# Maxima products of the first attention as four 32-query products on column tiles, for either row half

## The reference, cut to what matters

```python
scores = jnp.einsum('bhqd,bhkd->bhqk', q, k) / SCALING
att = jax.nn.softmax(scores, axis=-1)
out = jnp.einsum('bhal,bhlv->bhav', att, v)
```

## Time and profile before

| | |
|---|---|
| median of 3 runs | 1328.86 us (1328.58 to 1329.69) |
| the profiled execution | 1327.18 us, its span 1325.14 us |
| PE, share of the span busy | 91% |
| DVE | 75% |
| ACT | 63% |
| POOL | 20% |
| scores, L725, first to last start | 116.2 to 769.4 us |
| maxima, L614, first to last start | 95.2 to 743.0 us |

### The profile page before, as it was taken

How to read it: one execution, slowest core, us unless ns; L and a number is a source line. 1 busy time by engine, 2 the same in 40 slices (tenths; PEclk the granted TensorE clock), 3 DMA queues, 4 the chain that set the end, 5 groups by cost and what they waited for, 6 DMA issues and landing times. The chain is left out here.

```text
span 1325.1 us, 32172 instructions
## 1 busy us (share of the span) xinstructions
PE 1204.9 (91%) x13377; PEld 607.5 (46%) x13377; DVE 999.6 (75%) x1256; ACT 837.6 (63%) x1447; POOL 260.2 (20%) x373
## 2 busy tenths in 40 slices
PE   6977999999999999999999978888899799899980
PEld 4641333333323232233323345555799566688870
DVE  5879999999999999999999546765775788433324
ACT  3643888888888888888888845565222466533331
POOL 4200220000101001000010011100573222145560
PEclk9986999999999999999999989998998899999995
DMA  4764123232233322323311112000010211223317
GB/s 144 204 203 98 28 67 75 46 78 66 58 81 82 69 66 57 81 54 65 80 43 73 74 54 61 23 17 17 18 45 28 71 37 36 60 79 102 103 41 193
DMA packets 75229, 95.36 MB, mean 72 GB/s; under 512 B 13236, under 2 KB 44684, under 8 KB 74052
## 3 DMA queue, kind: packets, MB, share of 16 engines
q1 hardware_dynamic: 69996, 83.19, 24.4%
q0 software_dynamic: 5088, 10.12, 2.5%
HBM read 54.30 MB, written 38.56 MB: 70 GB/s over the span
## 5 line engine op out<-in xcount | busy, mean ns | idle before, releaser
L614 DVE TENSOR_REDUCE b_mx<-psum 128x2 f32<-128x1024 f32 x507 | 596.0, 1219 | 36.7 <-PE psum L558 27.9
L668 ACT ACTIVATE b_exp_ring<-psum 128x512 f32<-128x512 f32 x1024 | 540.0, 598 | 121.6 <-PE psum L725 120.8
L725 PE MATMUL psum<-b_q,b_k 75*32 75x512 bf16 x4096 | 315.4, 384 | 1.3 <-ACT b_exp_ring L668 1.1
L699 PE MATMUL psum<-b_exp_ring,b_v 128*32 128x512 f32 x2048 | 266.3, 595 | 0.7 <-ACT b_exp_ring L668 0.7
L557 PE MATMUL psum<-b_k,b_q 64*128 64x512 bf16 x512 | 188.4, 396 | 21.8 <-DVE b_mx L614 12.2
L558 PE MATMUL psum<-b_ko,b_qo 64*128 64x512 bf16 x512 | 188.4, 396 | 0.0
L725 PEld LDWEIGHTS psum<-b_q,b_k 75*32 75x32 bf16 x4096 | 86.5, 95 | 173.6 <-ACT b_exp_ring L668 112.3
L557 PEld LDWEIGHTS psum<-b_k,b_q 64*128 64x128 bf16 x512 | 47.3, 93 | 229.8 <-issue 132.7
L744 POOL CAST b_top<-b_mt 16x128 bf16<-16x128 f32 x32 | 8.9, 279 | 574.5 <-DVE b_mt L622 574.5
L1839 ACT ACTIVATE e_hT<-psum,e_b 128x358 f32<-128x358 f32 (+3 forms) x96 | 53.6, 559 | 75.4 <-PE psum L1859 72.0
L699 PEld LDWEIGHTS psum<-b_exp_ring,b_v 128*32 128x32 f32 x2048 | 60.8, 111 | 55.7 <-issue 9.6
(11 more groups left out here) (279 smaller groups left out, 1457.2 us busy)
## 6 DMA issues: line engine op xcount, KB each, us to landing
b_q<-q_ops SPq DMA_DIRECT2D x48, 192.0 KB
b_k<-k_ops SPq DMA_DIRECT2D x48, 192.0 KB
k_ops<-a_k SPq DMA_DIRECT2D x20, 256.0 KB, 3.4
x_disp<-b_zeros SPq DMA_DIRECT2D x13, 320.0 KB
e_x<-x_disp SPq DMA_DIRECT2D x8, 520.0 KB
v_ops<-a_vs SPq DMA_DIRECT2D x4, 1024.0 KB, 5.1
b_v<-v_ops SPq DMA_DIRECT2D x16, 256.0 KB
av_out<-b_acc SPq DMA_DIRECT2D x128, 32.0 KB, 1.7
```

The costliest lines, as they stand in the source:

```text
L614: nc.vector.reduce_max(mx[:, d % 2, :, i // 2, i % 2], pair, AX.X).then_inc(sem("b_max_done"), 1)
L668: act.activation(ex[:, n % E_RING, :], g.bank(5 + n % 3), ACT.Exp, scale=ATT_SCALE)\
L699: last = nc.tensor.matmul(AV[32 * i:32 * i + 32, :], v[s][:, at_v:at_v + 32], ex[:, (4 * group + i) % E_RING, :], start=(kb == 0), stop=(k ...
L725: last = nc.tensor.matmul(g.bank(5 + n % 3)[keys, :], k[s][0:XROWS, h, kb * P + 32 * j:kb * P + 32 * j + 32], q[s][0:XROWS, h, half * BANK ...
```

## The change

Both products of an item are cut by queries: each becomes four products of 32 queries, whose results lie on 32 partitions each of the same bank. The first four take the even head (row half 0), the next four the odd head (row half 64). The last one is returned, so the semaphore still counts one for an item. The streamed operand of 512 keys is the same for the four.

```diff
 def maxima_scores(g, q, k, qo, ko, n, p, i):
 
-    t, keys = slice(i // 2 * P, i // 2 * P + P), slice(i % 2 * BANK, i % 2 * BANK + BANK)
-    g.nc.tensor.matmul(g.bank(2 * (n % 2)), q[0:MROWS, 2 * p, t], k[0:MROWS, 2 * p, keys], start=True, stop=True)
-    return g.nc.tensor.matmul(g.bank(2 * (n % 2) + 1), qo[MROWS:P, p, t], ko[MROWS:P, p, keys], start=True, stop=True)
+    keys = slice(i % 2 * BANK, i % 2 * BANK + BANK)
+    tiles = ((q[0:MROWS, 2 * p, :], k[0:MROWS, 2 * p, keys]), (qo[MROWS:P, p, :], ko[MROWS:P, p, keys]))
+    for head, (qh, kh) in enumerate(tiles):
+        for j in range(STRIPS):
+            t = i // 2 * P + 32 * j
+            last = g.nc.tensor.matmul(g.bank(2 * (n % 2) + head)[32 * j:32 * j + 32, :], qh[:, t:t + 32], kh,
+                                      start=True, stop=True)
+    return last
```

## The result

The changed kernel takes 1336.76 us (median of 5 runs, 1335.52 to 1337.42), the kernel before 1329.42 us beside it (1328.58 to 1330.15): a ratio of 1.0055, with a 95% interval of 1.0040 to 1.0069. It is slower by 7 us, outside the 0.2% that a measurement of this kernel can tell. The forecast was 1333.8 us and slower; the sign and the range held, the size came out half as large again.

A forecast was written before the change was run, and what follows sets the result against it. The loop through PE and DVE over two blocks, 2.505 us a block, was taken as the bound. 245 blocks x 0.02 us = 4.9 us more, on the median of 1328.86, gave 1333.8 us, range 1320 to 1341.

The forecast's parts named there:

- The chain over two blocks: Loop through PE and DVE from B to B two blocks later, 5.01 us, 2.505 a block; taken as the bound.
- The switches of tile size: On PE between score and item products: each border costs 0.10 us extra, and the change saves nothing there.
- entry: PE step from a score group to an item's first product, forecast to stay at 0.31 to 0.32 us.
- exit: PE step from an item's last product to the next scores, forecast to stay at 0.31 to 0.32 us.
- Rivals 1 and 2: Tile-size switches on PE: 1, both go, 1310.8 us, chance 0.10; 2, one direction goes, 1321.5 us, chance 0.06.
- The row halves: Even and odd heads' products on PE: eight tiles in flight, their overlap costed at nothing.
- rival 3: On PE the row halves no longer overlap, second four start 0.22 us later: about 1415 us, chance 0.03.
- More instructions: Each item's last product starts six load-and-product pairs later, 3.3 ns each: 0.02 us, twice a chain, 4.9 us in all.
- rivals 4 and 5: Extra products: 4, dearer pairs, 7 to 28 ns, 1339 to 1370 us, chance 0.04; 5, starts hidden, 1328.9 us, 0.15.
- A: The first of a block's two maxima items; its maximum on DVE waits for its last product on PE.
- B: The second of a block's two maxima items; the next scores on PE follow its last product.
- the same two places: Before A's maximum and before the scores after B, 0.02 us each, also claimed for the 31 blocks with a transposition.

The follow-up runs named there:

- the larger memsets: Kernel before, with a memset of 144 columns on DVE ahead of each attention maximum: 1361.98 us, ratio 1.0245.

## Why the prediction was right, and where it fell short

**The bound.** Right. The chain over two blocks reads 5.01 us before and 5.07 after, as the medians of the pairs of blocks do, and 5.21 with the larger memsets, although PE and DVE on their own would need only 2.38 and 2.46 us a block there.

**The switches of tile size.** Right: entry 0.310 and exit 0.316 us, against 0.312 and 0.316 before. The prediction took this from switches between 128 and 32 rows at 128 columns, in f32, since no row had the pair itself. The pair is shown now: 64x32 beside 75x32 costs what 64x128 costs, and 72x32 beside it costs nothing. Rivals 1 and 2 fell with it. That 75 to 128 rows is free, the one row that spoke for rival 1, means that these count as one size, not that rows are free. The Trainium skill, TensorEngine Tiling (Array Packing), section Key Properties, has the drain go with the mode, and its list of configurations has 64x32 and 128x32 as two modes. The runs agree: the 0.10 us is there with 64x32 and not with 72x32.

**The row halves.** Right: the second four start 0.02 us behind the first four (408.38 and 408.40), so rival 3 fell.

**More instructions.** Right in the part that was costed: six pairs at 3.3 ns were to make 0.020 us, and the last product starts 0.020 us later (0.023 against 0.003). That it came out to the nanosecond is luck in part: the row's 0.01 us, at two decimals, allowed 0.01 to 0.03. So rivals 4 and 5, dearer pairs and hidden starts, fell as well.

**The step that was too small** is the next one, "It stands twice in the chain, since A's maximum waits for A's last product, and the scores after B for B's last. So 0.04 us a chain, 0.02 us a block." The scores after B do pay 0.020 us and no more. For A's maximum it took the way from the last product to DVE as fixed. It is not: it grew from 0.429 to 0.458 us, and A's first product to its maximum by 0.048 instead of 0.020. The chain gained 0.020 + 0.048 - 0.002 = 0.066 us, not 0.040. The pairs of blocks without a transposition gained 0.064. The pair with one gained some 0.03, although the prediction gave it the same two places and the whole price. The two misses work against each other: the average block gained 0.027 us, 6.6 us over 245 of them, where the first alone would have made 8.1. The prediction bounded the price of a pair from both sides, but as one price for both places; it had one row for this way, 0.43 us with two products, and set no bound on how it would change with eight. Why that way grows, by the number of products or by their width, stays open.

**The rest of the 7 us.** 6.6 us stand in the stretch of the scores. The ratio gives 0.55% of 1329 us, 7.3 us, with an interval of 5.3 to 9.2 us, and the remainder is within it.

**The alternatives.** None of the kernels beats the one before. Two products of 128 columns have the least to issue, a fast load and a short way to the maximum; what there is to gain are the 0.20 us of switches in each block. Giving items and scores one tile size removes them, but with 72 rows that costs a second pass; an order with fewer borders between items and scores was not tried.

## What to carry to other kernels

When products of two kinds alternate on PE, compare their tiles in both dimensions: rows and columns must fall in the same size (here 72, 75 and 128 rows counted as one, 64 did not), or, as in these runs, the start-to-start time at each border grows by some 0.10 us and the weights are not loaded ahead. Matching one dimension gave nothing back, and cutting a product into more tiles for it cost twice, at the last start and in the way to whoever waits for the result. Before pricing such nanoseconds, find out whether the place lies on a loop through two engines: there each step counts although neither engine is full.

## What the runs showed that I had not expected

The way from an item's last product to the engine that waits for it is not fixed: 0.417 us with 72x128, where one product starts alone, 0.429 with two of 64x128 or four of 72x32 together, 0.453 with four of 64x64, 0.458 with eight of 64x32, in either order. A load of 64 columns in bf16 is slower, 103 ns, than one of 128, 93 ns, so 64 is the worst of the three widths here for a load that can't run ahead. And a memset of 0.11 us ahead of a maximum lengthened DVE's step by 0.01 us only, while 80 columns more lengthened it by 0.08: what a short instruction costs in front of a long one can't be read from its own duration.
